# Row maxima turned to rows, two heads per 32 output rows, and key sums kept in PSUM, in a fused attention and expert kernel

## What is computed

```
q, k, v = h@Wq, h@Wk, h@Wv
lin: phi = [1, y, y_i*y_j (i<=j)] of y = q@Wqf (k@Wkf);  A = causal(phi_q phi_k^T)
     y = (A v + phi_q KV) / (A 1 + phi_q KS + 1e-6);  KV, KS: sums over earlier chunks of 128
win: softmax(q k^T / sqrt(8)) v over keys t-64 .. t
x = x + LN(x) + concat(lin, win) @ Wout
```

## Time and profile before

| | |
|---|---|
| median of 3 runs | 486.39 us (485.33 to 486.51) |
| the profiled execution: time, span | 485.23 us, 483.5 us |
| PE busy | 421.5 us, 87% of the span |
| DVE, ACT, POOL busy | 65%, 45%, 38% |
| mean granted clock of PE | 0.949 of full speed (2.4 GHz) |

### The profile page before, as it was taken

One profiled execution on the slowest core, in us unless ns is written; L12 is line 12 of the kernel. 1 busy time (PEld: TensorE's weight loads), 2 busy tenths in 40 slices (PEclk: granted clock), 3 DMA queues, 4 the chain that ended last, 5 costly groups with the idle time before them and its releaser, 6 DMA issues. The chain is left out here.

```text
span 483.5 us, 15295 instructions
## 1 busy us (share of the span) xinstructions
PE 421.5 (87%) x5093; PEld 294.4 (61%) x5093; DVE 313.9 (65%) x1289; ACT 215.2 (45%) x566; POOL 184.3 (38%) x320
## 2 busy tenths in 40 slices
PE   0887899999999999999999983299999999999930
PEld 0455677777777777777877762045555555555510
DVE  5475555777877778777787766446666666666614
ACT  1456455556455555555555540034444444434410
POOL 5254424435555455554545633202222222222220
PEclk9999899999999999999999995589999999999975
DMA  7548975445645555432222900211111111111008
GB/s 199 134 128 165 213 140 98 121 128 149 165 101 127 141 147 157 110 77 55 65 64 65 278 11 22 64 50 36 41 43 34 30 40 41 34 32 35 18 28 237
DMA packets 91630, 46.19 MB, mean 96 GB/s; under 512 B 56410, under 2 KB 89852, under 8 KB 91554
## 3 DMA queue, kind: packets, MB, share of 16 engines
q1 hardware_dynamic: 88562, 40.49, 34.3%
q0 software_dynamic: 2272, 4.46, 2.9%
q10 hardware_dynamic: 720, 0.26, 0.2%
HBM read 33.67 MB, written 11.98 MB: 94 GB/s over the span
## 5 line engine op out<-in xcount | busy, mean ns | idle before, releaser
L1303 POOL DMA_INDIRECT results<-qas,mrowid x39 | 38.3, 983 | 123.2 <-ACT qas L853 123.2
L1284 POOL TENSOR_SCALAR_AFFINE_SELECT amat<-amat 128x512 f32<-128x512 f32 x64 | 42.4, 662 | 100.2 <-ACT amat L793 99.6
L1076 DVE TENSOR_REDUCE mrow<-ps 128x4 f32<-128x512 f32 x64 | 44.0, 688 | 55.1 <-PE ps L585 55.1
L723 PE MATMUL ps<-wgl,rest 128*128 (+1 forms) x156 | 75.2, 605 | 2.9 <-DVE hT L1173 2.2
L806 ACT ACTIVATE pmat<-ps 128x512 f32<-128x512 f32 x64 | 38.2, 597 | 69.0 <-PE ps L640 69.0
L793 ACT ACTIVATE amat<-ps 128x512 f32<-128x512 f32 x64 | 38.2, 597 | 31.3 <-PE ps L597 31.3
L1173 DVE TENSOR_TENSOR hT<-ps,kv_tok 128x512 f32<-128x512 f32 x39 | 27.0, 691 | 26.6 <-PE ps L723 15.9
L723 PEld LDWEIGHTS ps<-wgl,rest 128*128 128x128 f32 x156 | 27.1, 193 | 25.5 <-issue 25.4
L708 PE MATMUL ps<-w,rest 128*128 (+1 forms) x78 | 41.9, 620 | 0.0
L640 PE MATMUL ps<-identb,mneg 128*128 128x128 bf16 x512 | 39.6, 220 | 0.0
L853 ACT ACTIVATE qas<-rest,mweight 128x128 f32<-128x128 f32 x39 | 15.7, 402 | 50.0 <-DVE rest L1190 50.0
(11 more groups left out here) (164 smaller groups left out, 921.7 us busy)
## 6 DMA issues: line engine op xcount, KB each, us to landing
qa_parts<-wgl SPq DMA_DIRECT2D x12, 256.0 KB, 3.5
ks<-k_parts SPq DMA_DIRECT2D x32, 96.0 KB
qas<-qa_parts SPq DMA_DIRECT2D x32, 96.0 KB
xin<-routed SPq DMA_DIRECT2D x39, 72.0 KB, 1.9
ks<-k_parts SPq DMA_DIRECT2D x32, 64.0 KB
qas<-qa_parts SPq DMA_DIRECT2D x32, 64.0 KB
w<-in_W SPq DMA_DIRECT2D x2, 1024.0 KB, 6.0
wgl<-in_Wg SPq DMA_DIRECT2D x2, 1024.0 KB, 6.1
```

Of the source, the lines that this page charges most:

```text
L723: t = mm(ps[:, GL, :], zxT[:, k % 2, s, :], rhs(wgl[:, bass.ds(e, 1), s, :]), start=(s == 0), stop=(s == 1))
L1076: v.tensor_reduce(mrow[:], ps[:, SQ, :].rearrange("p (a k) -> p a k", k=CH), AX.X, ALU.max).then_inc(max_done, 1)
L1284: q.affine_select(out=amat[:, u % 2], in_=amat[:, u % 2], compare_op=ALU.is_ge, fill=0.0, base=0, pattern=[[0, 4], [1, CH]], channel_multi ...
L1303: q.indirect_dma_start(results, bass.IndirectOffsetOnAxis(mrowid[:, m:m + 1], 0), yw[:, m, :], None, bounds_check=RESULTS - 1, oob_is_err= ...
```

## The change

1. **Maxima.** At the head of unit n PE multiplies `mneg` (128 x 8, stationary) by the identity, which gives 8 rows of 128 in a free part of an output bank (`maxima_turned`); ACT copies them to `mt` in bf16; where the eight products stood, four remain, each of a constant 8 x 128 one-hot matrix `sel` with `mt`. The wait for `mneg` moves to the head of the unit.
2. **Two heads per 32 output rows.** `v1` and `state` get slots in which two heads share 32 columns, with zeros beside them, so two units add into one output bank. ACT copies the bank after odd units only; four blocks a chunk are turned instead of eight, all at u=0; DVE normalizes both forms in one go of 256 columns.
3. **Key sums in PSUM.** They accumulate in the bank `KV` over the chunks of a sequence; DVE writes masked copies into one of two `state` buffers (one operation per unit, not two). The last chunk of each sequence makes no key sums and no key features.
4. **`post` is shorter.** Its steps of u=2 and u=3 move to u=1 and u=2, nothing of PE is left at u=3, and two rounds drain it, not three. For the last two chunks the router's places and weights come at u=3.
5. **Small edits.** Query features are two products of 256 columns, not four of 128; a fifth constant is loaded (`sel`, `epslin` for `keep`); loop code without registers.

```diff
+            def maxima_turned(n):
+                pair = n // 2
+                pe.wait_ge(mneg_ready, n + 1)
+                if pair + n % 2 > 1:
+                    pe.wait_ge(evac_done, pair + n % 2 - 1)
+                mm(ps[0:8, OUT0 + (n + 1) // 2 % 2, 2 * CH:3 * CH], mneg[:, n % 2].rearrange("p a k -> p (a k)"), identb[:],
+                   start=True, stop=True, skip_group_check=True).then_inc(mt_ready, 1)
...
+                    maxima_turned(n)
+                    pe.wait_ge(v1_ready, c + 1)
+                    if later:
+                        pe.wait_ge(phik_ready, kf + 1)
...
-                    pe.wait_ge(mneg_ready, n + 1)
...
+                    pe.wait_ge(mt_copied, n + 1)
                     for pr in range(4):
-                        for part in range(2):
-                            t = mm(ps[:, ST, pr * CH:(pr + 1) * CH], mneg[:, u % 2, part, pr:pr + 1].to_broadcast([128, 128]), identb[:],
-                                   start=False, stop=(part == 1), skip_group_check=True)
+                        t = mm(ps[:, ST, pr * CH:(pr + 1) * CH], sel[:, pr, :], mt[:, n % 2, :], start=False, stop=True, skip_group_check=True)
...
-                    for s in range(4):
-                        t = nc.tensor.transpose(ps[:, TR, s * CH:(s + 1) * CH], linT[:, 1 - p, s, :], ident[:])
-                    t.then_inc(t_lin, 1)
-                if u == 1 and has[1]:
-                    pe.wait_ge(norm_lin, c)
-                    for s in range(4):
-                        t = nc.tensor.transpose(ps[:, TR, s * CH:(s + 1) * CH], winT[:, 1 - p, s, :], ident[:])
-                    t.then_inc(t_win, 1)
+                    for k in range(2):
+                        nc.tensor.transpose(ps[:, TR, k * CH:(k + 1) * CH], linT[:, 1 - p, k, :], ident[:])
+                    for k in range(2):
+                        t = nc.tensor.transpose(ps[:, TR, (2 + k) * CH:(3 + k) * CH], winT[:, 1 - p, k, :], ident[:])
+                    t.then_inc(t_out, 1)
...
+                    act.wait_ge(mt_ready, n + 1)
+                    nc.scalar.copy(mt[:, n % 2, :], ps[0:8, OUT0 + (n + 1) // 2 % 2, 2 * CH:3 * CH]).then_inc(mt_copied, 1)
+                    if c:
                         post(c, u)
...
+                    if u % 2:
+                        bank, a = OUT0 + pair % 2, u // 2
+                        act.wait_ge(out_ready, n + 1)
+                        if c > 1:
+                            act.wait_ge(t_out, c - 1)
+                        nc.scalar.copy(linT[:, p, a, :], ps[:, bank, 0:CH])
...
+                        v.tensor_tensor(values4(state[:, (c + 1) % 2], u, 0, UD),
+                                        ps[0:PR, KV, 4 * u * UD:4 * (u + 1) * UD].rearrange("p (h f) -> p h f", f=UD),
+                                        statemask[:].rearrange("p (h f) -> p h f", f=UD), ALU.mult).then_inc(state_done, 1)
```

More of the change, by code:

```diff
@@ L25 @@
 FS = 48
+SLOTW = 288
 PR = 2 * FS
@@ L67, in constants @@
     c["statemask"] = sm.reshape(PR, 4 * UD)
-    keep = np.ones((128, NC + 1), np.float32)
-    keep[:, ::T // CH] = 0.0
-    c["keep"] = keep
+    sel = np.zeros((2, 4, 4, 128), np.float32)
+    for pr in range(4):
+        sel[:, pr, pr] = 1.0
+    slots = np.zeros((128, 2 * H), np.float32)
+    slots[:, :H] = EPS_LIN
+    c["epslin"] = slots
     q, kap = np.arange(WINDOW), np.arange(CH)
@@ L129, in build @@
         statemask = sb("statemask", [PR, 4 * UD])
-        keep = sb("keep", [128, NC + 1])
+        sel = sb("sel", [8, 4, 128], BF16)
+        epslin = sb("epslin", [128, 2 * H])
         norm_w = sb("norm_w", [D, 1])
@@ L549, in post @@
                         pe.wait_ge(r_logit, c - 2)
[L550 to L553, removed]
+                        pe.wait_ge(r_count, c - 2)
+                    if has[3] and c - 3 < NC - 2:
+                        positions(c - 3)
                     if has[1]:
-                        for s in range(2):
-                            t = nc.tensor.transpose(ps[:, TR, s * CH:(s + 1) * CH], att[:, s].rearrange("p h d -> p (h d)"), ident[:])
+                        for k in range(2):
+                            t = nc.tensor.transpose(ps[:, TR, k * CH:(k + 1) * CH], att[:, k * H:(k + 1) * H].rearrange("p h d -> p (h d)"), ident[:])
                     if has[2]:
@@ L571, in post @@
                     t.then_inc(wout_ready, 1)
+                if u == 3 and has[2] and c >= NC:
+                    if has[1]:
+                        pe.wait_ge(x1_ready, c)
+                    positions(c - 2)
             def window_scores(n, u, p, i):
@@ L600, in linear_scores @@
                     pe.wait_ge(phisq_done, n)
[L601 to L604, removed]
+                for par in range(2):
+                    t = mm(ps[0:PR, PHI, 0:2 * CH], sums[:, par, :], as_[:, p, 4 * u + par:4 * u + par + 3:2, :],
+                           start=par == 0, stop=par == 1)
@@ L605, in linear_scores @@
                 t.then_inc(phi_ready, 1)
+            def maxima_turned(n):
[5 more added lines that the diff above has]
+                   start=True, stop=True, skip_group_check=True).then_inc(mt_ready, 1)
             def chunk(c, p, i):
-                first = isinstance(c, int) and c == 0
+                later, kf = folded(c)
@@ L674, in _ @@
                 chunk(c, c % 2, c // 2)
-            for c in range(NC, NC + 3):
+            for c in range(NC, NC + 2):
                 for u in range(UNITS):
@@ L786, in post @@
                     nc.scalar.copy(catT[:, lo:hi].rearrange("p k t -> p (k t)"), ps[:, TR, lo * CH:hi * CH]).then_inc(cat_copied, 1)
+                if u == 3 and has[2] and c >= NC:
+                    gap_exp(c - 2)
             def squares(n, u):
@@ L799, in chunk @@
                     n = c * UNITS + u
-                    early = isinstance(n, int)
-                    j, hf = u // 2, u % 2
-                    bank = OUT0 + u % 2
-                    if not (early and c == 0):
+                    pair = n // 2
+                    act.wait_ge(mt_ready, n + 1)
+                    nc.scalar.copy(mt[:, n % 2, :], ps[0:8, OUT0 + (n + 1) // 2 % 2, 2 * CH:3 * CH]).then_inc(mt_copied, 1)
+                    if c:
                         post(c, u)
@@ L1026, in post @@
-                if u == 3 and (has[1] or has[2]):
+                if u == 0 and has[3] and c - 3 < NC - 2:
+                    weights_row(c - 3)
+                if u == 1 and has[3] and c - 3 < NC - 2:
+                    dve.wait_ge(cat_copied, c)
+                    places(c - 3)
+                if u == 2 and (has[1] or has[2]):
                     n = c - 1
-                    xc = x_all[:, bass.ds(c - 1, 1), :].rearrange("p a d -> p (a d)") if has[1] else None
+                    xc = x_all[:, c - 1, :] if has[1] else None
@@ L1066, in post @@
                         dve.wait_ge(r_oh, 2 * n)
-                        if not static or c > 2:
+                        if c > 2:
                             dve.wait_ge(pos_ready, n - 1)
                         v.tensor_tensor(member[:], onehot[:, 0], onehot[:, 1], ALU.add).then_inc(r_member, 1)
+                if u == 3 and has[2] and c >= NC:
+                    places(c - 2)
+                    weights_row(c - 2)
             def maxima(n, b, between=None):
@@ L1115, in chunk @@
+                    if n < UNITS * NC - 1:
+                        maxima(n + 1, (u + 1) % 2, next_state)
+                    if c:
                         post(c, u, p, i)
-                    if u == 1 and not (isinstance(c, int) and c == NC - 1):
+                    if u == 1 and c < NC - 1:
                         key_features(c + 1, 1 - p)
@@ new lines, in scatter_first @@
+            def scatter_first(r):
+                pool.wait_ge(r_slot, r + 1)
+                pool.wait_ge(r_row, r + 1)
+                pool.wait_ge(staged, r + 1)
+                if r == 0:
+                    pool.wait_ge(first_padded, 16)
+                scatter(r % 2, 0)
+            def post(c, u, p, i):
+                has = [0 <= c - k < NC for k in range(4)]
+                if u == 0 and 0 <= c - 4 < NC - 3:
+                    scatter(p, 1)
+                if u == 1 and has[3] and c - 3 < NC - 2:
+                    stage(c - 3)
@@ L1273, in post @@
                         scatter(1 - p, 1)
-                if u == 0 and (not static or 0 <= c - 4 < NC - 1):
+                if u == 3 and has[2] and c >= NC:
+                    stage(c - 2)
+                    scatter_first(c - 2)
                     scatter(p, 1)
             def chunk(c, p, i):
-                first = isinstance(c, int) and c == 0
                 for u in range(UNITS):
                     n = c * UNITS + u
-                    pool.wait_ge(square_done, computed(pool, n + 1))
+                    pool.wait_ge(square_done, n + 1)
```

374 lines of the change are left out of this document (179 added, 195 removed).

## The result

The changed kernel takes 544.6 us, median of four runs (540.8, 542.3, 547.0 and 615.0), against 485.9 for the kernel before on the same chip: a ratio of 1.119 with a 95% interval of 1.110 to 1.129. It is 12% slower, where the forecast was 470.8 us and faster.

What follows compares the result with a forecast made beforehand. PE was taken to bound attention, busy all 14.92 us of a chunk. Maxima -4.5, shared slots -7.3, key sums -3.5, first `mneg` +0.15 and tail -0.5 sum to -15.6 us: 470.8 us, 8-in-10 range 463 to 478.

Steps and rivals of the forecast that it cites:

- The step that failed: Maxima on PE: -0.22 us, turning product +0.056, shape step +0.10, about -0.07 a unit; -4.5 us over 64 units.
- A unit: Attention unit u=3, left without a step of `post`: 3.14 us on PE.
- The handover into and out of the 8 rows: Around the `sel` products on PE: another 0.10 us to enter the shape; leaving costs what leaving the eight old products does.
- the 0.43 named for the latter among the signs: Sign of being right: L651 starts 0.43 us after the first `sel` product.
- rival (a): `sel` products: no step for fewer rows, 64 x 0.10 = 6.4 us better, 464.4 us; chance 0.18.
- Transposes and key sums: PE: four of eight transposes go in 15 chunks, -7.3 us; key sums left out in two chunks, -3.5 us.
- u=0: First unit of a chunk on PE: 3.63 us, with 0.485 us of `post`.
- rival b: POOL's mask comes late: 0.45 us in 15 chunks give back 6.8 us, 477.6 us; chance 0.12.
- POOL's wait of 1.16 us: POOL's power waited 1.16 us for DVE; with its input one unit earlier it should not any more.
- `mneg`, `mt`, `att`: PE's inputs from DVE and ACT: all in time, except the first `mneg`, late by one wait, +0.15 us.
- Rival (c): PE stands at u=1 for `att`: slower, 490 us at 1.3 us a chunk; chance 0.05.
- The tail: Stretch up to the last scatters: one drain round less about -1.4, later weights about +0.9; taken as -0.5 us.

Runs made afterwards that it cites:

- e1: The changed kernel with part 1 alone undone (eight full products from `mneg` per unit again): 481.9 us, ratio 0.993.
- e2: The kernel before with part 1 alone put in, its four products having 8 rows: 640.1 and 645.5 us, ratio 1.32.
- e3: The changed kernel with `sel` and `mt` padded with zeros to 128 rows: 473.7 us, ratio 0.975.
- e7: The changed kernel with `sel` and `mt` of 64 rows, 8 real and 56 of zeros: 541.4 and 542.8 us, ratio 1.121.
- e5: The changed kernel with twelve dense bf16 products run once on PE at the head of the second unit: 483.4 us, ratio 0.999.
- e10: The changed kernel with the maxima as before (eight broadcast products) and POOL's first scatter moved from u=3 to u=2: 476.6 us, ratio 0.984.
- the padded kernel: The kernel of e3: the changed kernel with `sel` and `mt` padded with zeros to 128 rows, 473.7 us.
- e9: The padded kernel with POOL's first scatter of a chunk issued in u=2 instead of u=3: 465.4 us, ratio 0.962.
- e6: The changed kernel with the key-sum products made in chunks 7 and 15 as well: 627.5 and 627.6 us.

## Why the prediction was wrong

**The step that failed** is the one by which part 1 changed "only PE time": -0.22 us for four products fewer, +0.056 and +0.10, all priced at 2.4 GHz. The clock was no term of the sum and no rival. The profile of before could have raised the question: the level falls for 3.5 us in slice 5, so that execution depends on its coming back, and I never asked what PE must do for that. e1, e2, e3 and e7 show that the few rows of these products are the cause; e5, which falls as after does (51.3 us) and comes back with the burst, shows that it is the return and not the fall. It cost 64 us. The Trainium skill (TensorE: Matmul & The Clock Gate, Part 1) says that activity of PE releases the throttle, and warns of idle gaps; by that rule PE, never idle, would have been back as soon as in before. The trace differs: 163.9 us busy without a gap, all at 1.2 GHz.

**Point by point**, at the full clock:
- *A unit*: forecast 3.14, measured 3.14. The handover into and out of the 8 rows is as forecast (L672 to L676 0.34, L676 to L688 0.32; the 0.43 named for the latter among the signs doesn't follow from the prediction's own 4 x 0.056 + 0.10); with the turning product L656 starts 0.39 to 0.42 after L705 (0.42 from 239.97 to 240.39), where it took 0.37, so it costs 0.02 to 0.05 and not 0.056. So rival (a), no step for fewer rows, is out.
- *Transposes and key sums*: u=1 is 3.54 and u=2 3.80, as the steps of `post` on 3.14 give. e10 has parts 2 to 5 without the stall at 476.6, against 474.9 by the forecast's terms.
- *u=0*: forecast 3.63, measured 4.18. The move of the power was followed as far as POOL's mask (rival b), and it was even said that POOL's wait of 1.16 us would go. What then starts earlier was not asked: a scatter, on top of the output product whose signal ACT's copy waits for. Term missed: 0.5 us a chunk, 6.4 us in the padded kernel.
- *`mneg`, `mt`, `att`*: no waits, as forecast, but for 0.74 us at the first `mneg` (forecast 0.15) and 0.3 us once at `mt`. Rival (c), the slower one, was about `att` and did not come.
- *The tail*: forecast -0.5, measured +0.5.

The mechanism of the gain was right, its size too large. The forecast gain of 15.6 us and the handover that the zeros save (64 x 0.12 = 7.7) would make 23.3 us. Against the kernel before on the same chip the padded kernel gains 11.9 us, and 18.3 with the scatter moved, which the prediction did not have. In e9 the tail (0.6; 282.69 - 265.38 = 17.31 us), the first `mneg` (0.6) and u=0 (3.58 where 3.51 were due, 1.1 in all) make nearly half of the 5 us that are left; the rest was not traced down.

**Left open**: what exactly brings the level back; why chunk 7 brings it back in some executions and only chunk 15 in others; how POOL's DMA delays PE's signals, and why not in the kernel before.

## What to carry to other kernels

Where a profile shows a fall of the granted clock, ask of every edit of PE's work whether the clock will still come back; products that address few rows of the array can keep it down for good, though they take the same time. Zeros up to 128 rows cost PE nothing here and saved a change of shape; one dense burst behind the fall worked too. And when a wait goes on an engine off the critical path, look at what its next instruction will now start on top of; here it was a DMA of POOL on top of a signal of PE.

## What was not expected of the hardware

- PE 100% busy at 1.2 GHz for 163.9 us (after), 351.6 us (32 rows, one execution), 389.4 (e2) and 375.5 (e6), while the same instructions keep 2.4 GHz once they have it (129.7 us in after, 228.7 in e5):

```profile
53.10:404.70 351.60, 351.60 (x3712) 243.34 (x3711) 138.31 (x688) 125.85 (x342) 101.98 (x215) 0.50 0.30 81
```

- With 120 rows of zeros the traced executions keep 2.4 GHz all through attention: it isn't the values that matter.
- Beside an indirect DMA issued by POOL (1.07 us) PE's signals can be posted 0.2 to 1.4 us behind the recorded end of their products (mostly under 0.9), so that ACT starts 0.7 us later than without it and DVE 0.3 us; in after no signal of another engine is late, and in the kernel before PE's aren't either.
